# Attention: the second unit of pieces moved between a position's two pairs of scores

## The reference

```python
qkv = x @ w_qkv
Q = apply_rope(Q)
K = apply_rope(K)
attn = jnp.einsum('bqhd,bkhd->bhqk', Q, K) * scale
attn = jnp.where(causal, attn, jnp.asarray(NEG_INF, attn.dtype))
attn = jax.nn.softmax(attn, axis=-1)
out = jnp.einsum('bhqk,bkhd->bqhd', attn, V).reshape(B, S, dim)
```

## Time and profile before

| | |
|---|---|
| median of 3 runs | 3397.8 us (3395.02 to 3398.94) |
| profiled execution | 3396.45 us, of which span 3394.7 us |
| attention stage in it, about | 400 to 2058 us |
| one full group | 101.3 us |
| PE, DVE, ACT busy over the span | 86%, 76%, 46% |

### The profile page before, as it was taken

One profiled execution on the slowest core, in us unless ns is written; L12 is line 12 of the kernel. 1 busy time (PEld: TensorE's weight loads), 2 busy tenths in 40 slices (PEclk: granted clock), 3 DMA queues, 4 the chain that ended last, 5 costly groups with the idle time before them and its releaser, 6 DMA issues. The chain is left out here.

```text
span 3394.7 us, 63091 instructions
## 1 busy us (share of the span) xinstructions
PE 2929.7 (86%) x22564; PEld 1636.2 (48%) x22564; DVE 2576.0 (76%) x4840; ACT 1558.3 (46%) x2096; POOL 882.6 (26%) x1098
## 2 busy tenths in 40 slices
PE   5885479999999999999999996883999999788888
PEld 3553123332333333333333324772888888677776
DVE  3885788899888889888889833765677777566666
ACT  1443046666666666666666672110444444211111
POOL 1775001110111111111111111665233222233333
PEclk8998579999999999999999998775999999899999
DMA  2676311211121211121211104664455445322222
GB/s 69 186 202 175 77 28 50 56 36 46 47 57 47 56 38 44 48 56 47 58 38 44 36 8 116 201 191 161 156 157 161 153 153 158 110 93 93 93 93 74
DMA packets 385872, 315.06 MB, mean 93 GB/s; under 512 B 112636, under 2 KB 372200, under 8 KB 385640
## 3 DMA queue, kind: packets, MB, share of 16 engines
q1 hardware_dynamic: 373352, 278.44, 28.9%
q0 software_dynamic: 12288, 33.57, 3.0%
HBM read 194.27 MB, written 116.92 MB: 92 GB/s over the span
## 5 line engine op out<-in xcount | busy, mean ns | idle before, releaser
L871 ACT ACTIVATE probs<-ps_s 128x1024 f32<-128x1024 f32 (+3 forms) x1280 | 1078.0, 896 | 646.9 <-PE ps_s L1030 646.3
L895 DVE TENSOR_REDUCE piece_rest<-ps_m 128x1 f32<-128x512 f32 (+3 forms) x1344 | 799.8, 646 | 105.2 <-PE ps_m L1005 50.0
L895 DVE TENSOR_REDUCE piece_late<-ps_m 128x1 f32<-128x512 f32 (+2 forms) x960 | 586.5, 666 | 59.8 <-PE ps_m L1005 28.7
L1030 PE MATMUL ps_s<-q_st,k_st 50*128 50x512 bf16 (+7 forms) x5120 | 594.4, 346 | 17.8 <-ACT probs L871 15.2
L1045 PE MATMUL ps_o<-probs,vs 128*32 128x512 f32 (+3 forms) x5120 | 600.6, 541 | 9.2 <-POOL probs L851 7.5
L851 POOL TENSOR_SCALAR_AFFINE_SELECT probs<-probs 128x256 f32<-128x256 f32 x512 | 205.0, 406 | 1522.0 <-ACT probs L871 1516.8
L996 PE MATMUL ps_m<-k_st,q_st 48*128 48x512 bf16 (+3 forms) x2560 | 449.6, 364 | 165.6 <-DVE piece_rest L895 79.2
L996 PEld LDWEIGHTS ps_m<-k_st,q_st 48*128 48x128 bf16 x2560 | 114.6, 93 | 781.6 <-DVE piece_rest L895 386.5
L1030 PEld LDWEIGHTS ps_s<-q_st,k_st 50*128 50x128 bf16 (+1 forms) x5120 | 224.5, 95 | 249.0 <-ACT probs L871 90.8
L1753 ACT ACTIVATE act_g<-ps_g 128x512 f32<-128x512 f32 x117 | 69.9, 597 | 279.2 <-PE ps_u L1845 279.2
L1790 DVE TENSOR_TENSOR hid_f<-act_g,ps_u 128x512 f32<-128x512 f32 x117 | 80.5, 688 | 126.4 <-ACT act_g L1753 126.4
(11 more groups left out here) (226 smaller groups left out, 5016.7 us busy)
## 6 DMA issues: line engine op xcount, KB each, us to landing
qk_parts<-parts SPq DMA_DIRECT2D x128, 192.0 KB, 2.8
k_st<-qk_parts SPq DMA_DIRECT2D x768, 32.0 KB, 1.9
q_st<-qk_parts SPq DMA_DIRECT2D x768, 32.0 KB, 1.9
x_r<-expert_rows SPq DMA_DIRECT2D x39, 512.0 KB, 4.4
expert_made<-made SPq DMA_DIRECT2D x39, 512.0 KB, 2.9
x_in<-in_L_attn_x_dram SPq DMA_DIRECT2D x32, 512.0 KB, 4.5
v_ones<-v_out SPq DMA_DIRECT2D x64, 256.0 KB, 4.7
vs<-v_ones SPq DMA_DIRECT2D x64, 256.0 KB, 3.8
```

The costliest lines, as they stand in the source:

```text
L871: act.activation(probs[:, u % PSLOTS, 2 * pair:2 * pair + 2, j * P:ST], ps_s[:, pair, :, j * P:ST], ACT.Exp, scale=SCALE).then_inc(exp_don ...
L895: v.tensor_reduce(dst, ps_m[:, bank, 0:n * w].rearrange("p (n w) -> p n w", n=n), AX.X, ALU.max) \
L1030: last = pe.matmul(ps_s[:, pair, z, j * P:ST], k_st[rows, slot, half, pair, kc * P:(kc + 1) * P], q_st[rows, slot, half, pair, qt * ST + j ...
```

## The change

The call for the second slot moves from behind the loop over the two pairs into it, behind pair 0. The order at a position becomes: first slot, scores of pair 0, second slot, scores of pair 1, values. Nothing else is touched: the same instructions, the same waits, the same plan.

```diff
@@ -1070,7 +1070,8 @@
                             if pair == 0:
                                 pe.wait_ge(max_in[1 - par][0], (it + 1 + par) * (16 * MAX_DMAS))
                             scores(g + 1, 0, 1 - par, pair)
-                    some(todo[2 * u + 1])
+                        if pair == 0:
+                            some(todo[2 * u + 1])
                     values(g, u, par)
 
             for unit in numbered(PROLOGUE)[0]:
```

## The result

The changed kernel takes 3542.06 us (median; 3538.45 to 3546.74) against 3398.37 us for the kernel before: 1.0426 times as long, 95% interval 1.0408 to 1.0444. The forecast was 3539.

The account below looks back on a forecast made before the run. TensorE and VectorE were both nearly full in the attention, units spaced by VectorE's bank release; 9.4 us a group times 15 gave 141 us on 3396.45, about 3539 as median, with 8 in 10 for 3498 to 3572.

Parts of the forecast that it names:

- The law of the release: Attention: with three banks and two per unit, two units can't start closer than 0.42 + 0.61 + 0.14 = 1.17 us.
- The ordinary position: Position with both slots filled and 512-wide scores: 2.92 us against 2.49, +0.43, bounded between 0.31 and 0.52.
- the second half: From second unit to next first unit: TensorE, not VectorE, decides by 0.12 us, so nothing takes the loss back.
- that rival: Stall hidden in part: next first unit waits for VectorE and pair 1 fills that wait; 3498 us, chance 8%.
- The 23 positions: Positions with both slots filled and 512-wide scores: 23 x 0.43 = 9.9 us a group; short diagonal units spare 0.4.
- Turned outputs: "turn o" at 3, 17, 29 and 37 goes ahead of pair 1 with its slot: 0, at most +0.1 us each.
- The 384-wide three: Positions 12, 24 and 32, next scores 384 wide: a pair of 0.33 leaves its shadow, 3 x 0.33 = 1.0 us.
- Where it gains: Positions 0, 16 and 28: second slot fits the hole behind pair 0; -0.7, -0.3, -0.6, together -1.6 us a group.
- Left as they were: The six positions without a second unit, and 35 and 39 too, were to stay unchanged.
- The clock: Rival: TensorE standing once a position drops the granted clock; 4094 us, or 3594 for a tenth, chance 4%.
- The sum: All terms: 9.9 + 1.0 + 0.5 - 0.4 - 1.6 = 9.4 us a group, times 15 = 141 us.
- The rival on the other side: Second unit held only by TensorE's order starts at once behind pair 0; faster, 3329 us, chance 3%.

Follow-up runs that it names:

- The two shortened reductions: VectorE's reductions read half or a quarter of each piece's columns, in the changed kernel's order: 3405.49 and 3349.47 us, against 3322.93 and 3306.99 in the old order.
- the fills on VectorE: Both orders, with VectorE also filling 256 columns of a scratch tile behind each reduction: an ordinary group takes 120.0 us in the old order, 120.7 in the new.
- the run with the three positions alone: Kernel before, with the second slot behind pair 0 only at positions 0, 16 and 28: 3396.41 against 3413.18 us, ratio 0.9946.
- the run with 27 added: Second slot behind pair 0 at positions 0, 16, 28 and also 27, otherwise the old order: group 100.19 us, against 100.13 without 27.
- quartered reductions: Each reduction reads only a quarter of its piece's columns, a part of the maxima left out: 3349.47 us in the changed order against 3306.99 in the old.

## Why the prediction was right, step by step

- **The law of the release**, 0.42 + 0.61 + 0.14 = 1.17 us from unit to unit, held: 1.18 in the changed kernel. The two shortened reductions moved it to 0.91 and 0.77, and TensorE's other distances in the position stayed.
- **The ordinary position**, forecast 2.92 and +0.43, measured 2.93 and +0.44. That the second half takes nothing back, since TensorE decides there, held too; the fills on VectorE show the case in which it would have. (The price of that rival adds up to 3497 and not 3498, which changes nothing.)
- **The 23 positions**, forecast 9.9 less 0.4 for short units, 9.5: measured 9.8. The short units at 8, 20 and 21 spared 0.3 in sum, not 0.4. At 15 and 27, 0.1 each was spared that I had not seen: pair 0 behind them waited for ScalarE before, and the later values fill that wait. Turned outputs, taken at 0, cost +0.1 each at 3, 17 and 29: the values behind them used to follow the turn, and now follow bf16 scores, with the step of 0.10.
- **The 384-wide three**, forecast 1.0, measured 1.0; 34, 37 and 38, forecast 0.5, measured 0.6.
- **Where it gains**, forecast -0.7, -0.3 and -0.6, measured -0.63, -0.30 and -0.83. At 28 I had left the reductions of 27's unit where they stood in the old trace (1037.53), though 27 is itself changed. That gave a unit 1.02 us behind pair 0, which is what the run with the three positions alone shows; it is 0.75 in the changed kernel, and the run with 27 added shows the 0.27 us that come of it.
- **Left as they were**, said of 35 and 36 among others: in fact 35 is 0.44 shorter and 36 is 0.44 longer. The values of 35 are short, and the first unit of 36 stands 1.16 us behind the unit of 35 in either kernel, by the law of the release; it comes sooner because that unit does. In 36 the chain runs over ScalarE and GpSimd: pair 1 waits 0.20 us for ScalarE, the values 0.16 us for GpSimd's mask. What the first gains is only waited for in the second, and the sum was right without my having seen it, which is luck.
- **The clock** stayed at 1.00 with TensorE 97.04 / 111 = 87% busy, as worked out. The rule of the Trainium skill ("TensorE: Matmul & The Clock Gate", A second HAM failure mode: psum-queue depth-cycling), by which idle times between groups of matmuls that cycle through PSUM banks can make the clock oscillate, did not act in the changed kernel: idle times of 0.34 us once in 2.93 us for some 1,660 us left it at its upper level. The kernels with fills are the case in which the clock does go up and down (13 and 3 stretches at the lower level); so this rival was nearer than the changed kernel alone shows.
- **The sum**: forecast 9.4 a group and 141 us, measured 9.6 and 144.7, of which 1.1 and 1.1 us came back ahead of and behind the fifteen groups. The positions that lose came to 0.4 us a group more than forecast and those that gain to 0.2 more, and these partly cancel: that the forecast was 3 us off is closer than its terms were.

The rival on the other side, a second unit that doesn't wait, was to decide at a release below 0.65 us. No run reached this: with quartered reductions it is 0.77, and the moved order still loses 2.9 us a group there. That it would win below 0.65 is argued, not shown, except where no first unit stands, and there it does win.

## What to carry to other kernels

With three buffers and a unit that takes two, the distance between two units has a floor: hand-over, one reduction, hand-back (1.17 us here). Work between them is free up to that floor, so it should be spread to meet the floor on both sides; moving a block out of a gap that it just fills into one that is already full costs its whole length, though no instruction is added. Whether it costs anything at all depends on which engine is the bound in the gap that receives it: 0.2 us more of VectorE work per item turned +9.6 us a group into +0.7, at the price of longer single waits on TensorE, beside which its clock fell now and then. And where a gap has nothing to wait for (no first unit), the same move is a gain, so a rule for all positions should be split by what stands in front.

## What the runs showed of the hardware that I had not expected

With VectorE as the bound and the moved order, TensorE's clock went to its lower level for 3.4 or 6.8 us at a time, 13 times in some 1,830 us, 12 of them at positions 1, 27 and 28, and back each time. The page of that run doesn't show it, as every slice of the attention behind its start still reads nine tenths or more; the unequal lengths of the groups do.

The part behind the last maxima, from the last nmax_rest to the end, has the same code in all kernels, with the last group's turns apart. It took 1415.3 and 1414.2 us in the first two profiles, 1426.2 to 1434.1 us in the next eight kernels, which shared a chip, and 1415.1 and 1418.5 us in the last two, which shared another; the median of the kernel before was 3398.37, 3413.18 and 3399.06 us beside them. So the runs on one chip were about 14 us longer, as much as one of the effects studied here; whether the chip itself or something else of that session did it isn't shown. Within a profile, meanwhile, most groups agree to 0.02 us (12 of 14 in the kernel before), and plain positions take 2.49 us in the unchanged order on either chip. Effects of a few tenths of a per cent had to be read from the period of a group, or against a run of the kernel before on the same chip.
